# Testing four edge tiles at once for openings in two segment-sum loops on TensorE

## The chip, the cores and the metric

The kernel runs on one core of a Trainium2 chip, as one launch. The metric is the device time of that launch in microseconds. The time of the kernel before is the median of three runs.

## What is computed

A graph layer pair and a routed feed-forward over 3,125 nodes with 768 features and 50,000 edges that are sorted by destination. Two attention layers (eight heads, then one) each gather a row of features for every edge, scale it by the edge's softmax weight and add it up by destination; this sum is what the change touches. The rest is dense. The reference, cut to that:

```python
def gat_layer(x, W, a_src, a_dst, bias, src, dst, heads, out_c, concat):
    h = (x @ W).reshape(n, heads, out_c)
    e = jax.nn.leaky_relu(al_s[src] + al_d[dst], NEG_SLOPE)
    m = jax.ops.segment_max(e, dst, num_segments=n)
    ex = jnp.exp(e - m[dst])
    z = jax.ops.segment_sum(ex, dst, num_segments=n)
    msg = h[src] * (ex / (z[dst] + 1e-16))[:, :, None]
    out = jax.ops.segment_sum(msg, dst, num_segments=n)      # the two aggregations
    return out + bias

x = x + gat_layer(elu(gat_layer(layernorm(x), ..., heads=8)), ..., heads=1)
x = x + routed_ffn(layernorm(x))                             # top 2 of 8 experts
```

## The kernel before

The kernel is a row of parts that follow each other: setup, features, products and scores, `aggregate` (layer one, 8 heads), features and products of layer two, `aggregate_rows` (layer two), the routing and the experts.

Both aggregations work alike. The 50,000 edges are padded to NT = 392 tiles of 128 edges, taken in TURNS = 28 turns of UN = 14 tiles. POOL gathers the 128 rows of a tile by their source numbers into one of 14 buffers (L1473, L1664); it may issue the gather of tile t when TensorE has finished tile t - 13 (the semaphore tile_mm). In `aggregate` VectorE scales the gathered rows by the softmax weights (L1503), which TensorE waits for; in `aggregate_rows` ScalarE puts the weight into the one-hot matrix (L1924, L1931), and TensorE waits for the rows themselves.

TensorE adds a tile up with a one-hot matrix of 64 destinations: `sums` (L1526, L1820) makes two products with f32 operands, one for each half of the row, into one of two banks of accumulators. The 3,200 destinations are 50 groups (windows) of 64. Since edges are sorted, a tile mostly lies in one group. Where a tile reaches into the next group, it opens it: the tile is added once with the old group's one-hots into the old bank (`added`) and once with the next group's into the other bank (`opened`, which also waits for the flush of that bank). In `aggregate_rows` an opening into bank 0 issues besides the router's products (L1845) and the transposes (L1852) of a finished block of 128 destinations.

Which tile opens a group depends on data, so TensorE's sequencer branches. Once per turn it reads a word of 14 bits, `open_bits`, one bit per tile (L1568, L1889). Then the 14 tiles are taken in seven pairs (L1570 and L1891, the loop over k in steps of 2, written out in code). A pair without an opening (L1571: mask and branch) reads the bank register (L1577), branches on it (L1578) and adds both tiles. A pair with an opening reads three numbers of groups from `pair_ends` (L1572, L1893) and runs `single` for both tiles (L1552 to L1565), which has its own branches for the bank and for the groups to open. The same lines stand in `aggregate_rows` some 320 lines further down (L1888 to L1905). The loop over the turns is `pe.Fori` (L1567, L1888): a loop of the sequencer, with one copy of its body in the program.

Of the kernel before, what the change touches and what calls it, by code (L numbers as in the profile page):

```python
# [12 lines left out]
UN = 14  # L13
# [97 lines left out]
def gnn_ffn(nc, io, out):  # L111
    with ExitStack() as ctx:
# [1338 lines left out]
        def aggregate():  # L1451
# [13 lines left out]
            with nc.Block() as block:  # L1465
                @block.gpsimd
                def _(pool):
                    nc.gpsimd.memset(zeros, 0.0).then_inc(zero_set, 1)
                    for t in range(NT):
                        k = t % UN  # L1470
                        if t >= UN:
                            pool.wait_ge(tile_mm, t - UN + 2)
                        pool.indirect_dma_start(rows[k], None, feat_tab[0],  # L1473
                                                bass.IndirectOffsetOnAxis(ap=src_t[:, t:t + 1], axis=0)).then_inc(row_in[k], 16)
# [45 lines left out]
                @block.tensor  # L1520
                def _(pe):
                    def sums(hot, k, bank, start):

                        row = rows[k]
                        for c in range(WPB):
                            m = nc.tensor.matmul(acc[c * WIN:(c + 1) * WIN, bank, 0:HALF], hot, row[:, c * HALF:(c + 1) * HALF],  # L1526
                                                 start=start, stop=True, skip_group_check=True)
                            if c == 0 and not start and k % BATCH == 0:
                                m.then_inc(batch_mm, 1)
                        return m  # L1530

                    def added(i, k, bank):
                        if k % BATCH == 0:
                            pe.wait_ge(hot_ready, i * 2 + (k // BATCH + 1))
                        pe.wait_ge(msg_ready, i * UN + (k + 1))
                        sums(onehot[:, k, :], k, bank, False).then_inc(tile_mm, 1)

                    def opened(b, k, bank):
                        pe.wait_ge(open_ready, b)
                        pe.wait_ge(flushed, b)  # L1540
                        sums(next_x[bank], k, bank, True).then_inc(open_mm, 1)
                    pe.wait_ge(zero_set, 1)
                    for c in range(WPB):
                        m = nc.tensor.matmul(acc[c * WIN:(c + 1) * WIN, 0, 0:HALF], zeros[:, 0:WIN], zeros[:, 0:HALF], start=True, stop=True,
                                             skip_group_check=True)
                    m.then_inc(open_mm, 1)
                    bits_reg = [pe.alloc_register("bits0")]
                    regs = [pe.alloc_register(f"open0_{j}") for j in range(3)]
                    bank_reg = pe.alloc_register("bank0")
                    pe.reg_mov(bank_reg, 0)  # L1550

                    def single(i, k, b0, b1):  # L1552
                        bank = pe.snap(bank_reg, min_val=0, max_val=1)
                        with pe.If(bank > 0):
                            added(i, k, 1)
                        with pe.Else():
                            added(i, k, 0)
                        with pe.If(b1 > b0):
                            with pe.Fori(b0 + 1, b1 + 1) as b:
                                pe.reg_mov(bank_reg, b & 1)  # L1560
                                bank = pe.snap(bank_reg, min_val=0, max_val=1)
                                with pe.If(bank > 0):
                                    opened(b, k, 1)
                                with pe.Else():
                                    opened(b, k, 0)  # L1565

                    with pe.Fori(0, TURNS) as i:  # L1567
                        pe.load(bits_reg, open_bits[0:1, ds(i, 1)])  # L1568
                        bits = pe.snap(bits_reg[0], min_val=0, max_val=(1 << UN) - 1)
                        for k in range(0, UN, 2):  # L1570
                            with pe.If((bits & (3 << k)) > 0):  # L1571
                                pe.load(regs, pair_ends[0:1, ds(i * (UN * 4) + k * 4, 3)])  # L1572
                                b0, b1, b2 = [pe.snap(r, min_val=0, max_val=NW - 1) for r in regs]
                                single(i, k, b0, b1)
                                single(i, k + 1, b1, b2)
                            with pe.Else():
                                bank = pe.snap(bank_reg, min_val=0, max_val=1)  # L1577
                                with pe.If(bank > 0):  # L1578
                                    added(i, k, 1)
                                    added(i, k + 1, 1)  # L1580
                                with pe.Else():
                                    added(i, k, 0)
                                    added(i, k + 1, 0)
                    nc.tensor.matmul(tps[0:32, 0, 0:1], iota_f[:, 0:32], iota_f[:, 0:1], start=True, stop=True,
                                     skip_group_check=True).then_inc(open_mm, 1)

# [31 lines left out]
        def aggregate_rows():  # L1618
# [36 lines left out]
            with nc.Block() as block:  # L1655
# [158 lines left out]
                def _(pe):  # L1814
                    def sums(hot, k, bank, start):

                        row = rows[k]
                        for c in range(WPB):
                            n = CHUNK + ZC if c == WPB - 1 else CHUNK
                            m = nc.tensor.matmul(acc[c * WIN:(c + 1) * WIN, bank, 0:n], hot, row[:, c * CHUNK:c * CHUNK + n],  # L1820
                                                 start=start, stop=True, skip_group_check=True)
                            if c == 0 and not start and k % BATCH == 0:
                                m.then_inc(batch_mm, 1)
                        return m
# [31 lines left out]
                    bank_reg = pe.alloc_register("bank1")  # L1856
                    pe.reg_mov(bank_reg, 0)

                    def added(i, k, bank):
                        if k % BATCH == 0:  # L1860
                            pe.wait_ge(hot_ready, i * 2 + (k // BATCH + 1))
                        pe.wait_ge(row_in[k], i * 16 + 16)
                        sums(onehot[:, k, :], k, bank, False).then_inc(tile_mm, 1)
# [9 lines left out]
                    def single(i, k, b0, b1):  # L1873
                        bank = pe.snap(bank_reg, min_val=0, max_val=1)
                        with pe.If(bank > 0):
                            added(i, k, 1)
                        with pe.Else():
                            added(i, k, 0)
                        with pe.If(b1 > b0):
                            with pe.Fori(b0 + 1, b1 + 1) as b:  # L1880
                                pe.reg_mov(bank_reg, b & 1)
                                bank = pe.snap(bank_reg, min_val=0, max_val=1)
                                with pe.If(bank > 0):
                                    opened(b, k, 1)
                                with pe.Else():
                                    opened(b, k, 0)

                    with pe.Fori(0, TURNS) as i:  # L1888
                        pe.load(bits_reg, open_bits[0:1, ds(i, 1)])  # L1889
                        bits = pe.snap(bits_reg[0], min_val=0, max_val=(1 << UN) - 1)  # L1890
                        for k in range(0, UN, 2):  # L1891
                            with pe.If((bits & (3 << k)) > 0):
                                pe.load(regs, pair_ends[0:1, ds(i * (UN * 4) + k * 4, 3)])  # L1893
                                b0, b1, b2 = [pe.snap(r, min_val=0, max_val=NW - 1) for r in regs]
                                single(i, k, b0, b1)
                                single(i, k + 1, b1, b2)
                            with pe.Else():
                                bank = pe.snap(bank_reg, min_val=0, max_val=1)
                                with pe.If(bank > 0):
                                    added(i, k, 1)  # L1900
                                    added(i, k + 1, 1)
                                with pe.Else():
                                    added(i, k, 0)
                                    added(i, k + 1, 0)
                    pe.wait_ge(xT_ready, NW)  # L1905
                    pe.wait_ge(lg_ready, NW)
                    nc.tensor.matmul(tps[0:32, 1, 400:401], iota_f[:, 0:32], iota_f[:, 0:1], start=True, stop=True,
# [441 lines left out]
```

## Time and profile before

| | |
|---|---|
| time before, median of 3 runs | 2480.03 us (2477.85 to 2483.07) |
| the profiled execution's own time | 2465.81 us |
| its span, first to last instruction | 2464.0 us |
| PE busy, share of the span | 1854.5 us, 75% |
| PEld (weight loads, beside PE) | 985.7 us, 40% |
| DVE busy | 1299.3 us, 53% |
| ACT busy | 712.0 us, 29% |
| POOL busy | 1263.9 us, 51% |
| mean granted TensorE clock | 0.910 |

An engine counts as busy while it executes; register, branch, semaphore and DMA-issuing instructions of the sequencer are not counted. They are in the trace nonetheless, and stand under PEldq for TensorE's sequencer. A matmul's end is modelled. [...]

### The profile page before, as it was taken

The page shows a single profiled execution, that of the slowest core. Times are in us where ns is not written, and L with a number is a line of the kernel's source. Part 1 is how long each engine was busy: PE and PEld are TensorE (multiplying, and loading weights), DVE is VectorE, ACT ScalarE, POOL GpSimd, SP SyncE. Part 2 cuts the span into 40 slices and gives each one's busy share as a digit, 9 for nine tenths or more (in the row PEclk, how much of TensorE's full clock was granted, in tenths as well). Part 3 has the DMA queues.
Part 4 walks back from the last instruction along what each step waited for, and adds up shares of the span by engine and source line. Part 5 has one row for each costly group of instructions (what it writes and reads, how often), then busy time and mean ns, then how long its engine had stood idle before and what let it go on. Part 6 is the DMA issues. An engine that isn't in the chain of part 4 may idle for free. (4 is left out here: it accounts for less than half of the span.)

```text
span 2464.0 us, 32168 instructions
## 1 busy us (share of the span) xinstructions
PE 1854.5 (75%) x8856; PEld 985.7 (40%) x8857; DVE 1299.3 (53%) x2790; ACT 712.0 (29%) x1713; POOL 1263.9 (51%) x1279
## 2 busy tenths in 40 slices
PE   1847887957777777666979867777787784799997
PEld 1325554522222222224635432333333232677775
DVE  7725676836676766667647722343443436422221
ACT  1524433220010001015423333443443441133332
POOL 5065554036666666641051135666666661377775
PEclk9968998978999999897989988999989987899999
DMA  5322321158888888879569978999999986588886
GB/s 177 118 60 57 96 68 43 46 195 288 288 290 289 295 292 284 286 257 290 157 171 289 276 208 274 326 314 312 320 314 320 316 309 227 143 139 135 141 139 103
DMA packets 171459, 533.03 MB, mean 216 GB/s; under 512 B 35106, under 2 KB 66061, under 8 KB 171123
## 3 DMA queue, kind: packets, MB, share of 16 engines
q0 software_dynamic: 99088, 379.24, 53.9%
q1 hardware_dynamic: 61490, 123.21, 14.4%
q10 hardware_dynamic: 10800, 29.70, 3.0%
q8 instruction: 28, 0.46, 0.1%
q14 instruction: 53, 0.43, 0.1%
HBM read 444.94 MB, written 87.10 MB: 216 GB/s over the span
## 5 line engine op out<-in xcount | busy, mean ns | idle before, releaser
L1526 PE MATMUL acc<-ring,work 128*64 128x388 f32 x880 | 206.2, 552 | 83.3 <-issue 55.0
L1820 PE MATMUL acc<-ring,work 128*64 128x384 f32 (+1 forms) x880 | 192.5, 547 | 78.6 <-issue 78.3
L1664 POOL DMA_INDIRECT ring<-feat_tab,src_t x196 | 186.8, 953 | 107.5 <-issue 46.9
L951 PE MATMUL acc<-wg,work 128*128 128x384 f32 x600 | 223.8, 517 | 22.8 <-issue 14.4
L1931 ACT ACTIVATE work<-big,edges 128x64 f32<-128x64 f32 x392 | 135.9, 427 | 345.6 <-DMA edges<-in_w_slow 199.4
L1473 POOL DMA_INDIRECT ring<-feat_tab,src_t x196 | 185.2, 945 | 97.8 <-issue 49.0
L1778 DVE COPY work<-acc 64x384 f32<-64x384 f32 x100 | 56.0, 560 | 310.0 <-DMA ring<-lo_rows 253.5
L2140 POOL DMA_INDIRECT out_rows<-ring,wg x114 | 177.7, 1559 | 79.7 <-ACT ring L2237 56.7
L1503 DVE TENSOR_TENSOR ring<-ring,mps 128x776 f32<-128x776 f32 x196 | 182.9, 959 | 45.7 <-DMA ring<-feat_tab,src_t 33.1
L900 POOL DMA_INDIRECT edges<-score_tab,src_p x152 | 147.9, 973 | 113.2 <-issue 45.4
L1606 ACT ACTIVATE work<-acc 64x388 f32<-64x388 f32 x100 | 48.8, 488 | 514.6 <-DMA edges<-in_a_dst 489.7
L1284 PE MATMUL acc<-wg,work 128*128 128x384 f32 x504 | 184.8, 510 | 9.2 <-issue 7.2
L1526 PE MATMUL acc<-work 128*64 128x388 f32 x504 | 125.0, 548 | 59.9 <-issue 37.5
L1526 PEld LDWEIGHTS acc<-ring,work 128*64 128x64 f32 x880 | 65.4, 147 | 223.5 <-issue 162.4
L951 PEld LDWEIGHTS acc<-wg,work 128*128 128x128 f32 x600 | 114.9, 202 | 90.1 <-issue 34.4
L1820 PE MATMUL acc<-work 128*64 128x384 f32 (+1 forms) x504 | 116.6, 520 | 39.6 <-issue 38.8
L2274 DVE TENSOR_TENSOR edges<-acc,wg 128x192 f32<-128x192 f32 x57 | 20.4, 358 | 238.0 <-PE acc L2174 120.1
L1820 PEld LDWEIGHTS acc<-ring,work 128*64 128x64 f32 x880 | 67.6, 147 | 193.3 <-issue 185.5
L1664 POOL DMA_INDIRECT work<-feat_tab,src_t x112 | 106.5, 951 | 56.5 <-issue 26.9
L1473 POOL DMA_INDIRECT work<-feat_tab,src_t x112 | 105.8, 945 | 56.6 <-issue 26.2
L2174 PE MATMUL acc<-big,work 128*128 x684 | 123.5, 331 | 10.3 <-issue 9.1
L1284 PEld LDWEIGHTS acc<-wg,work 128*128 128x128 f32 x504 | 94.4, 197 | 66.5 <-issue 15.2
(393 smaller groups left out, 3500.7 us busy)
## 6 DMA issues: line engine op xcount, KB each, us to landing
ring<-lo_rows SPq DMA_DIRECT2D x49, 256.0 KB
edges<-in_w_slow SPq DMA_DIRECT2D x28, 384.0 KB, 9.6
edges<-in_w_hebb POOLq DMA_DIRECT2D x28, 384.0 KB, 7.7
edges<-in_w_fast POOLq DMA_DIRECT2D x28, 384.0 KB, 9.1
unit_sum<-edges SPq DMA_DIRECT2D x28, 384.0 KB, 6.7
out_rows<-work SPq DMA_DIRECT2D x52, 192.0 KB
feat_tab<-work ACTq DMA_DIRECT2D x25, 388.0 KB
agg_raw<-work ACTq DMA_DIRECT2D x25, 388.0 KB
```

The source lines that it names most:

```text
L900: pool.indirect_dma_start(src_s[:, t, :], None, score_tab, bass.IndirectOffsetOnAxis(ap=src_p[:, t:t + 1], axis=0)).then_inc(gather_in, 16)
L951: m = nc.tensor.matmul(acc[:, sl * 2 + c, 0:C // 2], xT[sl][:, k, :], wg[:, k, c * (C // 2):(c + 1) * (C // 2)], start=(k == 0), stop=(k = ...
L1284: m = nc.tensor.matmul(acc[:, sl * 2 + c, 0:C // 2], xT[sl][:, k, :], wg[:, k, c * (C // 2):(c + 1) * (C // 2)], start=(k == 0), stop=(k = ...
L1473: pool.indirect_dma_start(rows[k], None, feat_tab[0], bass.IndirectOffsetOnAxis(ap=src_t[:, t:t + 1], axis=0)).then_inc(row_in[k], 16)
L1503: V.tensor_tensor(r3, r3, ex_ps[i % 2][:, k, :].unsqueeze(2).to_broadcast([P, H, HC]), ALU.mult).then_inc(msg_ready, 1)
L1526: m = nc.tensor.matmul(acc[c * WIN:(c + 1) * WIN, bank, 0:HALF], hot, row[:, c * HALF:(c + 1) * HALF], start=start, stop=True, skip_group_ ...
L1664: pool.indirect_dma_start(rows[k][:, 0:C], None, feat_tab[1], bass.IndirectOffsetOnAxis(ap=src_t[:, t:t + 1], axis=0)).then_inc(row_in[k], 16)
L1778: ins = V.tensor_copy(r[w * WIN:(w + 1) * WIN, c * CHUNK:c * CHUNK + n], acc[c * WIN:(c + 1) * WIN, q % 2, 0:n])
L1820: m = nc.tensor.matmul(acc[c * WIN:(c + 1) * WIN, bank, 0:n], hot, row[:, c * CHUNK:c * CHUNK + n], start=start, stop=True, skip_group_che ...
L1931: ins = nc.scalar.activation(onehot[:, j * BATCH + k, :], gaps[j][:, k, :], ACT.Relu, bias=ex[:, first + k:first + k + 1], scale=neg_ex[:, ...
L2140: pool.indirect_dma_start(out[c], bass.IndirectOffsetOnAxis(ap=slots[:, 2, t:t + 1].bitcast(i32), axis=0), y_rows[t % TU][:, c * (C // 2): ...
L2174: m = nc.tensor.matmul(acc[:, 2, 0:HID], xTs[k][:, c, :], big[:, ds(e * HID + c * EH, HID)], start=(c == 0), stop=(c == KC - 1))
```

## The change

The seven pairs of a turn become three fours and a last pair, in both aggregations in the same way. A four is tested as a whole: the mask is 15 instead of 3. Where none of the four tiles opens a group, the bank is tested once and the four tiles are added in a row. Where one of them does, the two pairs are tested and run as before. The old code of the pairs is kept inside each four, and the code for four closed tiles, for either bank, comes beside it. No semaphore, wait or buffer is changed.

```diff
-                        for k in range(0, UN, 2):
+                        def pair(k):
                             with pe.If((bits & (3 << k)) > 0):
                                 pe.load(regs, pair_ends[0:1, ds(i * (UN * 4) + k * 4, 3)])
                                 b0, b1, b2 = [pe.snap(r, min_val=0, max_val=NW - 1) for r in regs]
                                 single(i, k, b0, b1)
                                 single(i, k + 1, b1, b2)
                             with pe.Else():
-                                bank = pe.snap(bank_reg, min_val=0, max_val=1)
-                                with pe.If(bank > 0):
-                                    added(i, k, 1)
-                                    added(i, k + 1, 1)
-                                with pe.Else():
-                                    added(i, k, 0)
-                                    added(i, k + 1, 0)
+                                inside(k, 2)
+
+                        def inside(k, n):
+                            bank = pe.snap(bank_reg, min_val=0, max_val=1)
+                            with pe.If(bank > 0):
+                                for t in range(k, k + n):
+                                    added(i, t, 1)
+                            with pe.Else():
+                                for t in range(k, k + n):
+                                    added(i, t, 0)
+                        for k in range(0, UN - 2, 4):
+                            with pe.If((bits & (15 << k)) > 0):
+                                pair(k)
+                                pair(k + 2)
+                            with pe.Else():
+                                inside(k, 4)
+                        pair(UN - 2)
```

The second hunk, in `aggregate_rows`, is the same text.

## Rows read from the trace of the kernel before

**Rows 1.** Windows: stretch and length us, busy us (count) per engine, PEclk, DMA share, GB/s.
```profile
556.00:1097.00 541.00, 394.09 (x1690) 123.95 (x1686) 376.13 (x451) 55.09 (x140) 349.65 (x370) 0.93 0.86 290
1480.70:1504.10 23.40, 14.98 (x60) 4.95 (x60) 1.34 (x3) 4.21 (x14) 11.22 (x12) 0.79 0.68 217
1504.10:1520.80 16.70, 14.59 (x84) 6.93 (x82) 7.58 (x23) 8.41 (x28) 10.50 (x12) 0.94 0.89 283
1520.80:2051.00 530.20, 408.16 (x2038) 177.66 (x2040) 222.14 (x627) 212.78 (x707) 338.69 (x355) 0.93 0.91 316
```

**Rows 2.** TensorE's sequencer by line: count, duration ns min/median/max, first and last start us.
```profile
L1568 PEldq TENSOR_LOAD <-open_bits x28: 3/307/678, 525.8 to 1081.3; - x28
L1889 PEldq TENSOR_LOAD <-open_bits x28: 5/308/1087, 1479.2 to 2035.1; - x28
L1571 PEldq ALU_OP  x196: 3/36/700, 526.4 to 1097.3; - x196
L1571 PEldq COMPARE_BRANCH  x196: 3/208/1283, 526.5 to 1097.4; - x196
L1577 PEldq MOVE  x147: 3/37/1392, 527.0 to 1095.9; - x147
L1578 PEldq COMPARE_BRANCH  x219: 2/169/2601, 527.1 to 1096.0; - x110
L1572 PEldq TENSOR_LOAD <-pair_ends x49: 13/755/1772, 541.2 to 1097.7; - x49
```

**Rows 3.** Timeline of PE at 1727 us: start us, length us, what.
```profile
1727.62 2.85 PE L1820 MATMUL acc<-ring,work 128*64 128x384 f32 x16 [1.59 <-issue]
```

**Rows 4.** Timeline of POOL, 1710 to 1723 us: start, length, gather, idle before and its releaser.
```profile
1710.34 0.94 POOL L1664 DMA_INDIRECT wg<-feat_tab,src_t  x1 [1.99 <-PE acc L1820]
1711.59 0.95 POOL L1664 DMA_INDIRECT edges<-feat_tab,src_t  x1 [0.31 <-issue]
...
1722.20 0.95 POOL L1664 DMA_INDIRECT ring<-feat_tab,src_t  x1 [2.16 <-DMA ring<-lo_rows]
```

**Rows 5.** Groups by line of PE and PEld: count, busy us, mean ns, idle us before.
```profile
L1526 PE MATMUL acc<-ring,work 128*64 128x388 f32 x880 | 206.2, 552 | 83.3 <-issue 55.0 <-DVE ring L1503 26.9 <-ACT work L1606 0.7
L1526 PE MATMUL acc<-work 128*64 128x388 f32 x504 | 125.0, 548 | 59.9 <-issue 37.5 <-DVE work L1503 17.9 <-DVE wg L1503 2.7
L1526 PE MATMUL acc<-edges,work 128*64 128x388 f32 x256 | 62.4, 525 | 13.4 <-issue 11.7 <-DVE edges L1503 0.8 <-ACT work L1606 0.7
L1526 PE MATMUL acc<-wg,work 128*64 128x388 f32 x124 | 36.5, 558 | 5.1 <-issue 4.5 <-DVE wg L1503 0.4
L1526 PEld LDWEIGHTS acc<-ring,work 128*64 128x64 f32 x880 | 65.4, 147 | 223.5 <-issue 162.4 <-DVE ring L1503 59.0
```

**Rows 6.** Queue q8: whole span; 0-556; 520-556; 1110-1506; 1479-1506; 2055-2464 us.
```profile
q8 instruction: 28, 0.46, 0.1%
q8 instruction: 11, 0.18, 0.2%
q8 instruction: 4, 0.07, 0.8%
q8 instruction: 13, 0.21, 0.2%
q8 instruction: 6, 0.10, 1.4%
q8 instruction: 4, 0.07, 0.1%
```

**Rows 7.** Sequencer branches, short windows at 537, 1480, 1495 and 1498 us: ns min/median/max.
```profile
L1578 PEldq COMPARE_BRANCH  x1: 2601/2601/2601, 537.8 to 537.8; - x1
L1892 PEldq COMPARE_BRANCH  x2: 337/2506/4674, 1479.8 to 1480.8; - x2
L1892 PEldq COMPARE_BRANCH  x1: 2377/2377/2377, 1495.1 to 1495.1; - x1
L1892 PEldq COMPARE_BRANCH  x1: 3502/3502/3502, 1498.2 to 1498.2; - x1
```

More of the change, by code:

```diff
@@ L1890, in _, with pair @@
                         bits = pe.snap(bits_reg[0], min_val=0, max_val=(1 << UN) - 1)
-                        for k in range(0, UN, 2):
+                        def pair(k):
                             with pe.If((bits & (3 << k)) > 0):
@@ L1897, in _, with inside @@
                             with pe.Else():
[L1898 to L1904, printed above, removed]
+                                inside(k, 2)
+                        def inside(k, n):
+                            bank = pe.snap(bank_reg, min_val=0, max_val=1)
+                            with pe.If(bank > 0):
+                                for t in range(k, k + n):
+                                    added(i, t, 1)
+                            with pe.Else():
+                                for t in range(k, k + n):
+                                    added(i, t, 0)
+                        for k in range(0, UN - 2, 4):
+                            with pe.If((bits & (15 << k)) > 0):
+                                pair(k)
+                                pair(k + 2)
+                            with pe.Else():
+                                inside(k, 4)
+                        pair(UN - 2)
                     pe.wait_ge(xT_ready, NW)
```

## The prediction

> **What bounds the kernel now.** I read four views in this order. The windows table gives the two aggregation stages: 541 us of the first one and 530 us of the second go by with POOL, DMA and TensorE all partly busy, none full [rows 1]. The sequencer's rows give the pace: the read of open_bits, one per turn of 14 tiles, runs from 525.8 to 1081.3 us and from 1479.2 to 2035.1 us, 28 times each, so a turn takes 555.5/27 = 20.6 us (the second likewise), 1.47 us per tile [rows 2]. TensorE's own work is far less: where nothing interferes it takes 16 matmuls, four tiles, in 2.85 us, 0.71 us per tile [rows 3]. POOL needs 1.25 us per gather (0.95 busy, 0.30 between), 17.5 us per turn, and makes up the rest of 20.6 us in pauses of about 2 us every eight gathers or so, here one that a TensorE matmul ended [rows 4]. So the pace is a ring: POOL waits for freed rows, TensorE frees them, and TensorE is held up while POOL's gathers run. It isn't TensorE's instruction count: the second stage ran 2,038 matmuls in 530 us, with the router's and the transposes' among them, the first 1,690 in 541 us, at the same pace [rows 1, 2].
> TensorE has a reserve. The second turn of stage two, which starts with rows waiting, took 16.7 us [rows 1]. So it can lose up to 20.6 - 16.7 = 3.9 us per turn before the ring must slow down.
>
> **The change, part by part.** The destinations are sorted, and 49 tiles open a group (the 49 reads of pair_ends [rows 2]), one in eight, so no four tiles hold two openings. Counted from the edge list, 8 of the 49 fall in the last pair of a turn, which keeps its old code; 41 of the 84 fours of each stage have an opening, 43 have none.
> Removed: a four without an opening loses one of two pair tests and one of two bank tests: a mask (36 ns), a branch (208), a move (37), and the bank's branch, at 219 records for 147 pairs, 1.49 times 169 ns [rows 2]. That is 0.53 us, times 43, 23 us per stage.
> Added: a four with an opening pays one more mask and branch and one jump over the other body, at most 36 + 208 + 169 ns = 0.41 us, times 41, 17 us per stage.
> What of it lies on the path: the sequencer runs ahead of the array over closed pairs (four tiles without a pause in [rows 3]), which hides the saving; the 0.41 us stands ahead of the 0.75 us register read [rows 2], where nothing hides it. The ends are all savings and no additions, -46 us for both stages, and the reverse, +34 us. I take -5 us, near nothing, because the pace didn't follow the instruction count above.
>
> The third part is not in the diff's words: **the loop body grows.** A tile's addition is 8 TensorE instructions, four loads and four matmuls (1,764 of each on L1526 for 392 tiles, 49 openings and no more [rows 5]), and one or two for its waits. Each four gets its own body for either bank, 2 x 4 x 9 instructions, with tests and jumps 78, or 80 where a wait for the one-hots falls in: 238 more per loop. The compiled program before has 995 instructions in the first loop and 1,499 in the second.
> What code size costs stands in the instruction queue: q8 brings TensorE's code: four packets in the first turn of stage one, six in that of stage two, 0.10 MB. The windows 0 to 556, 1110 to 1506 and 2055 to 2464 us hold 11 + 13 + 4 = 28, all there are, so none falls in the other 27 turns of either stage [rows 6]. A packet is 16 KB, 256 instructions: 28 packets for the 7,138 instructions, less what was loaded at the start [rows 6]. So code comes in blocks and stays. Where a branch goes to a block that isn't there, the sequencer stands: four branches of the two first turns took 2.60, 4.67, 2.38 and 3.50 us [rows 7], against 0.21 us as a rule [rows 2]. Their places in the program fix the block edges: at every 256th instruction, give or take three, from position 193. Loop two now runs from 4,676 to 6,175: blocks 4545 to 6081, seven of them; the sixth packet is then the block behind the loop, fetched ahead. So the store keeps eight blocks for 27 turns: seven of the loop and one unused.
> After the change loop two starts 238 later and is 238 longer: 4,914 to 6,651. It lies in eight blocks, 4801 to 6593, the last reached by 58 instructions, every turn, since the last pair's code stands there. With the block fetched ahead it wants nine. Loop one (1,950 to 3,183) has six and one ahead and fits.
> No row shows whether a ninth block is kept. If it is, the cost is one more first fetch per stage, 0 to 9 us. If not, the block fetched ahead displaces a block of the loop, most simply the oldest, which is its head, and each of 27 back jumps meets a missing block. The nearest rows price that at 2.38 to 4.67 us; if the head waits behind the block in flight, two in a row, up to 9.3 us [rows 7]. I take 5.6 us, above the middle, because the jump comes within a microsecond or so of entering the last block. Half is swallowed by the reserve of 3.9 us, which can't be all free since the ring also needs POOL's 17.5 us: 2.8 us per turn, times 27, +75 us; with none swallowed 9.3 x 27 = +250, with all 0.
>
> [...]
>
> **Rivals.** (a) *Fits, and the tests were on the path.* The ninth block is kept or not fetched; the saving of 0.53 us per closed four shows in part, 6 to 46 us over both stages. For it: PE's idle time before L1526 is mostly put down to its own issue [rows 5]. Time: about 2480 - 18 = 2462 us. This is the other side of my forecast, and the number of kept blocks decides it. (b) *Fits, and nothing moves:* the change hardly does what it says, because tests run ahead of the array, or the additions eat the saving: 2480 us. (c) *The store is a plain window of eight blocks:* the displaced head displaces the next on its return, and so on round the loop. A turn then meets four or five missing blocks (head, behind each closed four, last pair), 3.3 us on average [rows 7] to 4.67, about 17 us, less 3.9 of reserve: 13 us times 27, +350 us, range +220 to +520: 2830 us. For it: no row of code ever coming back. Against it: nothing either; it takes another rule for replacing. (d) *Forecast: one missing block per turn.*
>
> **Numbers.** Against the profiled execution's own 2465.8 us (its span is 2464.0): -5 (tests) + 3 (first fetches, mostly under the full ring) + 75 (back jumps) = +73 us, 2539. The median of the runs shown is 2480.0, 14 us above the profiled one; I carry that over: 2553 us. Chances: (d) 0.33, with its own range 2490 to 2700; (c) 0.27; (a) 0.25; (b) 0.13; fits but slower, since the additions are exposed, 0.02. The range takes in (d), (b), nearly all of (a) and half of (c): 2452 to 2840. The bound for faster or slower is 0.2%, 5 us, about what a measurement of this kernel can tell from no change: faster 0.25, same 0.13, slower 0.62.
>
> **What would show it.** Packets of q8 in turns 2 to 28 of stage two: about two per turn in (d), six to nine in (c), none in (a) and (b). The longest branches move to the loop's own back jump on the line of the Fori in stage two, at 2.4 to 9 us each, 27 times. Stage one keeps 20.6 us per turn within 0.5 us in all cases but (a), and serves as a control. Records of the pair's mask drop from 196 to 28 + 2 x 41 = 110 per stage, and as many as 84 new ones appear. The prediction fails outright if stage two has no packets after its first turn; its size is wrong if the reserve swallows all (no change at +5 us per turn) or none.

## The result, and the profile after

| | before | after |
|---|---|---|
| median of the runs taken together | 2481.55 us (2477.85 to 2485.82, 4 runs) | 2843.49 us (2842.65 to 2850.68, 4 runs) |
| ratio | | 1.146, 95% interval 1.1438 to 1.1482 |
| span of the profiled execution | 2464.0 us | 2841.6 us |
| mean granted TensorE clock | 0.910 | 0.839 |

The change makes the kernel 15% slower. Nearly all of the loss, 361 of 378 us of the span, falls in the second aggregation. The reads of open_bits, one per turn, of stage one (L1568) and of stage two (now L1899), with count, duration in ns (minimum, median, maximum), first and last start:

```profile
L1568 PEldq TENSOR_LOAD <-open_bits x28: 307/312/1114, 528.2 to 1087.4; - x28
L1899 PEldq TENSOR_LOAD <-open_bits x28: 307/312/849, 1488.7 to 2405.7; - x28
```

Against [rows 2], stage one takes 559.2/27 = 20.7 us per turn (before 20.6), stage two 917.0/27 = 34.0 us (before 20.6). The 27 turns cost 917.0 - 555.9 = 361 us more, 13.4 us each. The rest of the span's 378 us is 9.5 us up to the start of stage two (1488.7 against 1479.2) and 7 us behind its last read.

The code queue of the changed kernel, in the whole span and then in the windows 0 to 560, 1110 to 1485, 1485 to 1512 (the first turn of stage two), 1512 to 2430 and 2430 to 2842 us (packets, MB, share):

```profile
q8 instruction: 272, 4.46, 0.8%
q8 instruction: 12, 0.20, 0.1%
q8 instruction: 7, 0.11, 0.1%
q8 instruction: 6, 0.10, 1.7%
q8 instruction: 243, 3.98, 2.2%
q8 instruction: 4, 0.07, 0.1%
```

Two queues are of the kind "instruction". The other, before and after, in the whole span:

```profile
q14 instruction: 53, 0.43, 0.1%
q14 instruction: 52, 0.43, 0.1%
```

It has 52 or 53 packets in all thirteen runs. q8 has 27 to 30 or 271 to 273, and its count moves with TensorE's code alone: the two kernels of the experiments that differ by 60 of TensorE's instructions, none of them executed, have 28 and 271 packets of q8, and 52 of q14 each. So q8 is read here as the queue of TensorE's code. Each of its packets is 16 KB (4.46 MB / 272).

The whole program before had 28 packets and none in turns 2 to 28 [rows 6]. Now the part of stage two from its first back jump on holds 243, which is 27 x 9. Between 560 and 1110 us, in stage one, there is still none. Where TensorE's sequencer stands meanwhile, by line; L1898 is the loop's own back jump, L1902 the pair's test, L1912 the bank's, L1919 the four's. The last two rows are the pair's and the four's test in stage one, as a measure:

```profile
L1898 PEldq COMPARE_BRANCH  x28: 67/5233/7142, 1512.5 to 2430.2; - x28
L1902 PEldq COMPARE_BRANCH  x110: 67/217/5575, 1499.4 to 2426.1; - x110
L1912 PEldq COMPARE_BRANCH  x157: 65/192/4489, 1493.2 to 2425.5; - x157
L1919 PEldq COMPARE_BRANCH  x84: 68/3911/6345, 1489.3 to 2421.2; - x84
L1571 PEldq COMPARE_BRANCH  x110: 2/208/717, 543.1 to 1103.6; - x110
L1588 PEldq COMPARE_BRANCH  x84: 3/77/705, 528.9 to 1099.6; - x84
```

The 84 tests of a four fall into two kinds: 43 take 3.8 us or more, 41 some 0.08 us, and the median lies between them. 43 is the number of fours without an opening, whose test jumps over the pairs' code; in stage one such a jump takes some 0.2 us. The back jump has a median of 5.2 us. From the first back jump on, the branches over 1.5 us in stage two are 120 with 521.3 us (41 at the fours' test, 40 at a pair's, 27 back jumps, 12 others): 4.4 stalls per turn of 4.3 us each, 19.3 us per turn. Of these 13.4 show in the pace.

The engines, in windows over stage one and stage two (length, busy us and count of PE, PEld, DVE, ACT and POOL, then PEclk, DMA share, GB/s), which answer to [rows 1]:

```profile
560.00:1103.00 543.00, 390.68 (x1686) 127.08 (x1682) 377.16 (x449) 54.58 (x139) 349.67 (x369) 0.93 0.87 288
1485.00:2430.00 945.00, 508.62 (x2196) 248.96 (x2198) 236.80 (x670) 225.58 (x749) 359.33 (x379) 0.71 0.61 193
```

The same view of the kernel before, over the whole of its stage two:

```profile
1485.00:2055.00 570.00, 438.18 (x2193) 190.75 (x2193) 234.54 (x668) 225.41 (x749) 359.47 (x377) 0.93 0.89 309
```

Every engine has idle time. That PE was busy 509 us instead of 438 for as many matmuls is no more work, but a slower clock, as one turn shows. Timeline of PE (start, length, what, idle before it), and under it the windows over four stretches of that turn:

```profile
1781.86 1.71 PE L1830 MATMUL acc<-edges,work 128*64 128x384 f32 x8
1789.89 2.88 PE L1830 MATMUL acc<-ring,work 128*64 128x384 f32 x8 [6.32 <-issue]
...
1803.06 3.68 PE L1830 MATMUL acc<-ring,work 128*64 128x384 f32 x12 [2.90 <-issue]
1806.53 3.80 PE L1830 MATMUL acc<-work 128*64 128x384 f32 x20
1810.14 0.85 PE L1830 MATMUL acc<-wg,work 128*64 128x384 f32 x4
1818.09 2.88 PE L1830 MATMUL acc<-edges,work 128*64 128x384 f32 x8 [7.11 <-issue]
```
```profile
1789.90:1792.70 2.80, 2.80 (x8) 0.72 (x8) 0.00 (x0) 1.17 (x4) 0.95 (x1) 0.50 0.02 9
...
1806.60:1810.20 3.60, 3.52 (x24) 1.78 (x22) 1.34 (x3) 2.73 (x9) 2.69 (x4) 1.00 0.91 311
1818.10:1820.90 2.80, 2.80 (x8) 0.80 (x8) 0.00 (x0) 0.00 (x0) 0.95 (x1) 0.50 0.27 89
```

TensorE stands for 6.32 and for 7.11 us, and this view names "issue" alone for both. TensorE's sequencer stood in branches meanwhile, the back jump in the first gap, a bank's and a pair's test one after the other in the second (duration three times over, in ns, and start):

```profile
L1898 PEldq COMPARE_BRANCH  x1: 5542/5542/5542, 1781.8 to 1781.8; - x1
L1912 PEldq COMPARE_BRANCH  x1: 4489/4489/4489, 1809.5 to 1809.5; - x1
L1902 PEldq COMPARE_BRANCH  x1: 3605/3605/3605, 1814.1 to 1814.1; - x1
```

After each of the two gaps the granted clock is 0.50, and 8 matmuls take 2.88 us (0.36 us each). At 1.00, 20 take 3.80 us (0.19 us each). In [rows 3], 16 took 2.85 us (0.18 us each). So in this turn the matmuls behind a stall also ran at half the pace. POOL's part is seen in the largest group of its gathers in stage two, first before (1485 to 2055 us), then after (1485 to 2430 us). Its idle time, once about evenly "issue" and TensorE, now mostly ends with TensorE:

```profile
L1664 POOL DMA_INDIRECT ring<-feat_tab,src_t x188 | 179.1, 953 | 100.5 <-issue 44.8 <-PE acc L1820 40.6 <-DMA ring<-lo_rows 15.1
L1674 POOL DMA_INDIRECT ring<-feat_tab,src_t x189 | 179.2, 948 | 196.0 <-PE acc L1830 167.8 <-issue 19.8 <-DMA ring<-lo_rows 8.5
```

### The profile page after: what moved, and what is told of

The parts are those of the page before. It is cut to its first block and busy times, and to the rows that moved or that the text cites. A ratio compares the mean times of both kernels' runs of the same rounds, so it can differ in the third digit from the quotient of the medians.

```text
span 2841.6 us, 31925 instructions
## 1 busy us (share of the span) xinstructions
PE 1923.5 (68%) x8856; PEld 1048.3 (37%) x8857; DVE 1303.3 (46%) x2790; ACT 712.8 (25%) x1713; POOL 1262.8 (44%) x1279
## 3 DMA queue, kind: packets, MB, share of 16 engines
q8 instruction: 272, 4.46, 0.8%
## 5 line engine op out<-in xcount | busy, mean ns | idle before, releaser
L1830 PE MATMUL acc<-ring,work 128*64 128x384 f32 x880 | 251.8, 736 | 305.1 <-issue 305.1
L1830 PEld LDWEIGHTS acc<-ring,work 128*64 128x64 f32 x880 | 103.6, 200 | 445.1 <-issue 436.1
L1830 PE MATMUL acc<-work 128*64 128x384 f32 x504 | 124.5, 621 | 67.3 <-issue 67.2
L1674 POOL DMA_INDIRECT edges<-feat_tab,src_t x56 | 53.0, 947 | 233.0 <-PE acc L1830 228.2
L1526 PEld LDWEIGHTS acc<-ring,work 128*64 128x64 f32 x880 | 66.1, 150 | 233.8 <-issue 185.8
L951 PEld LDWEIGHTS acc<-wg,work 128*128 128x128 f32 x600 | 115.3, 202 | 96.4 <-issue 41.2
```

Of the source, the lines that this page charges most:

```text
L951: m = nc.tensor.matmul(acc[:, sl * 2 + c, 0:C // 2], xT[sl][:, k, :], wg[:, k, c * (C // 2):(c + 1) * (C // 2)], start=(k == 0), stop=(k = ...
L1674: pool.indirect_dma_start(rows[k][:, 0:C], None, feat_tab[1], bass.IndirectOffsetOnAxis(ap=src_t[:, t:t + 1], axis=0)).then_inc(row_in[k], 16)
```

## The experiments

The theory under test: the store for TensorE's code keeps eight blocks of 256 instructions. Loop two executes eight blocks after the change and fetches a ninth ahead, behind its end, and with nine wanted in a circle each is dropped before it is wanted again. The rival: the fours themselves cost the time, by their tests, branches or longer bodies, or any growth does. Positions below are counted in the compiled program, and block edges are taken at 193 + 256n, as the prediction read them from the four branches of [rows 7], give or take three; loop two of the changed kernel goes from 4,915 to about 6,635, 42 past the edge at 6,593. "Dead" instructions are matmuls in an `If` that is never entered, so they change the place of code, and add no more than one test per turn. Where that test is inside a loop, the bound of `bits` is widened by one bit for it (not shown). In the code shown, `...` stands for lines or parts of lines left out.

**The same changed code, moved by 168 instructions.** Dead code in front of loop two puts its head at 5,085, behind the edge at 5,057; it then lies in seven blocks, though it is as long as before.

```diff
+                    at_start = pe.snap(bank_reg, min_val=0, max_val=1)
+                    with pe.If(at_start > 0):
+                        for _ in range(42):
+                            nc.tensor.matmul(tps[0:32, 1, 400:401], iota_f[:, 0:32], iota_f[:, 0:1], start=True, stop=True, ...
                     with pe.Fori(0, TURNS) as i:
```

> The changed kernel, with 168 TensorE instructions that are never executed put in front of the second loop, so that its head moves from position 4,915 to 5,085 and its end to about 6,805. The loop is as long as in the changed kernel (some 1,720 instructions), but now lies in seven blocks (5057 to 6593) instead of eight. Theory A (the code store keeps eight blocks, the one fetched ahead counts): stage two falls back to 20.6 us per turn, no code packets after its first turn, 2475 to 2490 us. Rival B (the longer body or the tests and jumps themselves cost the time, wherever they lie): nothing moves, 2840 us. Rival C (the store holds fewer instructions than the body, by length alone): 2840 us too, with nine packets per turn. If A holds, this run is also the price of the tests alone in both stages: 0 to -30 us against the kernel before.

Measured: 2470.10 us against 2467.26 of the kernel before on the same chip, ratio 1.0012 (1.0003 to 1.0021). The whole loss is gone, with every four in place:

```profile
q8 instruction: 30, 0.49, 0.1%
L1904 PEldq TENSOR_LOAD <-open_bits x28: 3/308/1148, 1482.3 to 2040.0; - x28
```

557.7/27 = 20.66 us per turn. The rival falls: what cost 361 us was where the code lay.

**Dead code in the kernel before, 196 and 136 instructions.** Both have the old pairs and one jump over dead code in loop two. With 196 the loop ends at 6,373, past the edge at 6,337, in eight blocks; with 136 it ends at 6,313, in seven.

```diff
                         for k in range(0, UN, 2):
+                            if k == 6:
+                                with pe.If((bits & (1 << UN)) > 0):
+                                    for _ in range(49):                    # 34 in the other
+                                        nc.tensor.matmul(tps[0:32, 1, 400:401], iota_f[:, 0:32], iota_f[:, 0:1], start=True, stop=True, ...
```

> The kernel before with its pairs, and in the body of the second loop 196 TensorE instructions behind a branch that is never taken, with one more mask and branch per turn. The body now ends near 6,373, past the block edge at 6,337, by some 36 instructions: eight blocks and one ahead. A: 27 turns with nine missing blocks each, stage two 33 to 35 us per turn, 2800 to 2860 us, 244 code packets more. B (fours and their tests are the cause): 2480 us, since there are no fours. C (length alone, threshold unknown): either.

> As the run with 196 dead instructions, but 136 of them: the body ends near 6,313, 24 short of the block edge at 6,337, seven blocks. A: no packets after the first turn, 2475 to 2490 us. B: the same. C (length alone, growing with it): between the kernel before and the run with 196, nearer to that one.

Measured: with 196, 2884.28 us, ratio 1.1694 (1.1664 to 1.1724); with 136, 2469.49 us, ratio 1.0015 (1.0005 to 1.0025). The reads of open_bits and the queue, first with 196, then with 136:

```profile
q8 instruction: 271, 4.44, 0.7%
L1889 PEldq TENSOR_LOAD <-open_bits x28: 302/311/643, 1477.4 to 2437.6; - x28
```
```profile
q8 instruction: 28, 0.46, 0.1%
L1889 PEldq TENSOR_LOAD <-open_bits x28: 16/308/1128, 1476.6 to 2035.2; - x28
```

Sixty instructions that are never executed make 415 us: 35.6 us per turn against 20.7. The loss needs no four, and it isn't gradual. Its size is a little above what I expected (33 to 35 us per turn, at most 2860 us).

**The change in one stage alone.** Stage one alone keeps loop two as it was, in seven blocks; stage two alone ends its loop at about 6,397, in eight.

```diff
                         # in the other stage:
-                        for k in range(0, UN - 2, 4): ...
-                        pair(UN - 2)
+                        for k in range(0, UN, 2): ...
```

> The change in the first aggregation alone; the second has the kernel before's pairs again (its head at 4,915, its end near 6,413, seven blocks). Both A and B: no loss in stage two. A: 2475 to 2485 us, stage one 20.6 us per turn as in the kernel before. If the tests are on the path in stage one, 3 to 23 us less than before. B, where a longer body costs by itself: some us more than before.

> The change in the second aggregation alone. Its loop starts where the kernel before's does (4,677) and ends near 6,397, past the edge at 6,337: eight blocks and one ahead. Code store: nine packets per turn, 33 to 35 us per turn, 2820 to 2880 us, the whole loss of the changed kernel. If the loss came from the first stage's longer code or from both together: less than 2700 us.

Measured: stage one alone 2466.78 us, ratio 0.9998 (0.9989 to 1.0007); stage two alone 2824.47 us, ratio 1.1459 (1.1433 to 1.1484), 271 packets, 33.4 us per turn. Where the fours fit they are worth nothing, and where they don't the loss is there in full.

**What the tests are worth.** One kernel puts one more test, an `If` that is never entered, ahead of each pair of the kernel before, 392 in all. Another has the fours in both stages, but takes the pairs' own test out of a four with an opening (it runs four `single`), which makes the code about as long as before.

```diff
                         for k in range(0, UN, 2):
+                            with pe.If((bits & (1 << UN)) > 0):
+                                pe.sem_inc(open_mm, 0) if False else pe.reg_mov(bank_reg, 0)
```
```diff
                             with pe.If((bits & (15 << k)) > 0):
-                                pair(k)
-                                pair(k + 2)
+                                for j in (k, k + 2):
+                                    pe.load(regs, pair_ends[0:1, ds(i * (UN * 4) + j * 4, 3)])
+                                    b0, b1, b2 = [pe.snap(r, min_val=0, max_val=NW - 1) for r in regs]
+                                    single(i, j, b0, b1)
+                                    single(i, j + 1, b1, b2)
```

> The kernel before with one more mask and branch ahead of each pair in both loops (392 of each more, never taken, 0.04 + 0.08 to 0.21 us and the gaps between them), which doubles the pair tests. The second loop still lies in seven blocks. If tests are on the path: 392 x 0.25 to 0.35 = +100 to +140 us, and the change's fours would then be worth 10 to 20 us. If the sequencer runs ahead of the array, or the ring sets the pace: 0 to +10 us, and the fours are worth nothing.

> Fours in both loops, but a four with an opening runs all its four tiles as single ones with their own branches and two reads of the ends, without pair tests. The loops are as short as in the kernel before (the second from 4,659 to about 6,133, seven blocks), so nothing is refetched. Open fours cost some 2 us more of sequencer each (one more read at 0.75 us, two more single tiles at 0.6 us), 41 per stage, closed ones 0.5 us less, 43 per stage. If the sequencer is on the path: +60 to +120 us. If the ring sets the pace: within 10 us of before.

Measured: 392 more tests, 2473.41 us against 2466.77, ratio 1.0027 (1.001 to 1.0044): 6.6 us (2.5 to 10.9), 17 ns each. The added test's rows in stage one:

```profile
L1571 PEldq COMPARE_BRANCH  x196: 3/208/697, 525.6 to 1096.6; - x196
L1571 PEldq ALU_OP  x28: 11/36/712, 525.5 to 1082.6; - x28
```

The mask is taken only once per turn here, so that what each pair gained is the branch alone, which jumps over the body in 208 ns. Over 90% of that is hidden beside the ring. Fours with singles: 2469.31 us, ratio 1.0011 (0.9997 to 1.0025), against the +60 to +120 us that I expected if the sequencer were on the path.

**Does the store hold a window of the program, or any eight blocks?** Here 1,200 dead instructions stand inside loop one (and 36 ahead of it). The loop executes five blocks and, by the theory, fetches two ahead, seven in all, but they lie across ten.

```diff
+                            if k == 6:
+                                with pe.If((bits & (1 << UN)) > 0):
+                                    for _ in range(300):
+                                        nc.tensor.matmul(tps[0:32, 0, 0:1], iota_f[:, 0:32], iota_f[:, 0:1], start=True, stop=True, ...
```

> The kernel before with 36 dead instructions in front of the first loop and 1,200 more behind a never taken branch in the middle of its body (before tile 6), which the sequencer jumps over each turn. The loop lies from 1,988 to 4,184. It touches the blocks 1985 and 2241, jumps over four, and goes on in 3521, 3777 and 4033: five blocks, with those fetched ahead (2497 and 4289) seven; from first to last it spans nine, ten with the one ahead. Theory T (the store holds any eight blocks, by their addresses, and drops the one not used longest): no packets after the first turn, stage one 20.6 us per turn, 2475 to 2490 us. Theory W (a window of consecutive blocks that holds eight): the head is gone at every back jump, nine or ten packets per turn, stage one 30 to 38 us per turn, 2700 to 2950 us. Theory W' (a window, but a jump out of it fetches only what is wanted): four to seven packets per turn.

Measured: 2467.96 us against 2466.77, ratio 1.0011 (0.9998 to 1.0024).

```profile
q8 instruction: 29, 0.48, 0.1%
L1573 PEldq TENSOR_LOAD <-open_bits x28: 3/308/794, 528.0 to 1083.8; - x28
```

Stage one stays at 555.8/27 = 20.6 us per turn, without a packet between 560 and 1110 us. Two pairs of the loop's blocks lie exactly eight apart and don't displace each other. In this run it is the number of blocks that counts, not how far they reach or which place in the store they would share.

**Does a block that is only fetched ahead count?** 136 dead instructions ahead of loop two and 1,160 inside it: seven blocks are executed, and two more are never executed, but lie behind one that is left by a jump, one at the hole and one behind the loop.

> The kernel before with 136 dead instructions in front of the second loop and 1,160 more behind a never taken branch in its body (before tile 6). The loop lies from 4,814 to about 7,475. Each turn executes code of seven blocks only: 4801, 5057, 5313, then over the hole 6593, 6849, 7105, 7361. The blocks behind 5313 and behind 7361 (5569 and 7617) are never executed, only fetched ahead. Theory P (a block fetched ahead takes one of the eight places like any other): 7 + 2 = 9, so nine packets per turn, and stage two at 30 to 36 us per turn, 2720 to 2880 us. Theory U (only executed blocks hold their places, those fetched ahead give way first): none or two packets per turn, 20.6 us per turn, 2475 to 2490 us; under U the changed kernel would fail for its eight executed blocks, and the store would keep seven of them and one ahead.

Measured: 2671.84 us against 2225.28 us of the kernel before on the same chip, ratio 1.2008 (1.1906 to 1.211). The queue in the whole span, then in 1347 to 2270 us, and the two stages' reads:

```profile
q8 instruction: 273, 4.47, 0.7%
q8 instruction: 244, 4.00, 2.0%
L1568 PEldq TENSOR_LOAD <-open_bits x28: 308/314/1180, 455.9 to 934.6; - x28
L1894 PEldq TENSOR_LOAD <-open_bits x28: 307/312/575, 1319.4 to 2243.9; - x28
```

Nine packets per turn again, at 34.2 us per turn against 17.7 in stage one, though only seven blocks are executed. A block fetched ahead took a place like any other here, and was fetched anew each turn. The kernel before is itself 10% faster on this chip (a point for the last section), so the 2720 to 2880 us that I expected don't apply; against that kernel on the same chip the loss is 447 us.

**What sets the pace that hides the tests.** Two kernels leave out part of stage two: one takes half the columns in the matmuls of `added`, the other gathers as many pieces of half a row's length (384 elements, counted by the same numbers in a table of half rows).

```diff
-  m = nc.tensor.matmul(acc[..., bank, 0:n], hot, row[:, c * CHUNK:c * CHUNK + n],
+  m = nc.tensor.matmul(acc[..., bank, 0:n if start else n // 2], hot, row[:, c * CHUNK:c * CHUNK + (n if start else n // 2)], ...
```
```diff
-  pool.indirect_dma_start(rows[k][:, 0:C], None, feat_tab[1],
+  pool.indirect_dma_start(rows[k][:, 0:C // 2], None, feat_tab[1].rearrange("n (a c) -> (n a) c", a=2), ...
```

> Leaves out part of the computation: in stage two the matmuls of `added` take only half of their columns (192 of 384), so half of each sum is missing. Instructions, tests, waits and code length are those of the kernel before. Question: is the matrix work of TensorE in the 20.6 us per turn? If TensorE's array or the reading of its operands set the pace, stage two loses about 0.3 us per tile, 4 us per turn, 110 us in all, and a turn takes 16 to 17 us. If the pace is set by POOL's gathers and the way in which freed rows reach POOL, the turn stays at 20.6 us within 0.5 and the total within 15 us of the kernel before. I expect the second.

> Leaves out part of the computation: in stage two each gather fetches half a row (384 elements of 768), by the same number of gathers, so the other half keeps old values. Question: is the amount of data in the 20.6 us per turn? If the transfer of the rows is on the ring, a turn falls towards POOL's own 14 x 1.25 = 17.5 us, 3 us less, and stage two loses some 85 us; if only the number of gathers and the return of freed rows count, the turn stays at 20.6 us within 0.5. The stage moved 316 GB/s before; I expect a gain of 30 to 85 us.

Measured, on one more chip where the kernel before takes 2225.87 us: half the columns 2228.85 us, ratio 1.0013 (0.9999 to 1.0027); half the rows 2217.81 us, ratio 0.9954 (0.9937 to 0.9971). The reads of open_bits, half columns (stage one, stage two), then half rows (stage two):

```profile
L1568 PEldq TENSOR_LOAD <-open_bits x28: 302/309/1282, 457.1 to 938.4; - x28
L1889 PEldq TENSOR_LOAD <-open_bits x28: 302/317/1109, 1316.4 to 1797.0; - x28
```
```profile
L1889 PEldq TENSOR_LOAD <-open_bits x28: 302/309/1061, 1317.1 to 1788.2; - x28
```

A turn takes 17.8 us in both stages and 17.4 us with half the data: POOL's own 14 x 1.25 = 17.5 us [rows 4]. Half of the data gains 8 us of the 30 to 85 that I expected. Half of the columns gains nothing, but it didn't halve TensorE's time either. The windows 1320 to 1800 us, half columns, then half rows (whose matmuls keep all columns):

```profile
1320.00:1800.00 480.00, 354.26 (x2116) 216.47 (x2118) 228.24 (x644) 223.58 (x744) 354.71 (x372) 0.74 0.97 360
1320.00:1800.00 480.00, 391.90 (x2162) 175.23 (x2160) 230.07 (x649) 225.39 (x749) 359.51 (x378) 0.96 0.70 211
```

TensorE was busy for 354 us instead of 392, at a mean granted clock of 0.74 instead of 0.96. So this run tests 10% less of TensorE's time, not half of it. What speaks for POOL as the pace on this chip is that a turn takes what its 14 gathers take. The 3 us per turn more on the other chips weren't there to be taken apart, so what makes them stays open.

## Why the prediction was wrong

It had the mechanism and chose the wrong one of its two sizes. Point by point:

- **The ring and its pace:** right as a reading (20.6 us per turn), and right that TensorE's instruction count isn't in it: 392 tests more cost 6.6 us. That TensorE's freeing of rows makes the difference between 17.5 and 20.6 us was argued and isn't shown.
- **The tests, -5 us (ends -46 to +34):** stage one alone gave -0.5 us, both stages with the code moved out of the way +2.8 us (by the ratio 0.7 to 5.2), two code packets more included; before that run I had still expected 0 to -30 us. "Near nothing" held. The counts held too: 110 records of the pair's mask and 84 new ones per stage.
- **First fetches, +3 us:** one packet more outside turns 2 to 28 of stage two (29 against 28). Too small to be seen apart.
- **Where the code lies:** I put loop two at 4,914 to 6,651. It lies at 4,915 to about 6,635: the loop grew by 222 instead of 238. Still eight blocks, by 42 instructions instead of 58. This step held, and all hung on it.
- **Whether a ninth block is kept:** no row told, and the 0.60 that (c) and (d) have together was my estimate. For the case that it isn't: "most simply the oldest, which is its head, and each of 27 back jumps meets a missing block". The first half fits the nine packets per turn. The step that failed is the second, the term of **5.6 us per turn with half swallowed, 2.8 x 27 = +75 us**. It stopped after one displacement. But the head, when it comes back, displaces the block that is now the oldest, which is the next one wanted, and so on round the loop: with nine blocks wanted in turn and eight places, dropping the oldest misses all nine. The trace shows exactly nine packets per turn, and the term measured 13.4 us per turn, 13.4 x 27 = 361 us, instead of 2.8 and 75. One miss per turn would need a store that drops some other block than the oldest, and I had named the oldest myself.
- **The rival with that consequence** was rival (c), and its sum came within a few per cent: 17 us of stalls per turn, less 3.9 of reserve, 13 us times 27, 2830 us. Measured were 19.3 us of stalls, 5.9 swallowed, 13.4 us, 2843 us. The four or five stalls were 4.4, at 4.3 us (3.3 to 4.67 forecast). That it came so near is in part luck: the stalls and the part swallowed were both larger than I had them, and the two errors cancel. I called it a "plain window of eight blocks"; the run with the hole in loop one shows that it is no window, but any eight blocks. Its condition should have been read as "the store drops the oldest or least recently used block", which needs no further rule and deserved the larger chance.
- **The reserve of 3.9 us:** I took half of it as usable, and more than all was swallowed, 5.9 us. One turn was also a poor measure of it: in the trace of the kernel before the reads of open_bits in stage two lie 16.3 to 24.1 us apart, and a turn in the middle of the stage took 16.7 us too. The 5.9 us leave out the matmuls that ran at granted clock 0.50 behind the gaps (behind 53 of the 54 over 4 us between 1512 and 2430 us); TensorE was busy 509 - 438 = 71 us longer in stage two, 2.6 us per turn. How the pace divides between stalls and clock these runs don't separate.
- **The control:** stage one stayed within 0.2 us of 20.6 per turn, as said. Its loop has six blocks and one ahead.

The kernels whose loop executes seven and eight blocks, with one ahead, bear out the number eight: 28 q8 packets with 136 dead instructions, 271 with 196. Which block is dropped they don't show: a store that drops the one fetched first and a store that drops the least recently used both miss all nine in a circle.

The end of my range, 2840 us, was 3 us short because it took in only half of a case to which I gave 0.27, and cut it near its centre.

## What to carry to other kernels

Before a loop body of TensorE's sequencer is unrolled, specialised or given a second copy, count its blocks from the compiled positions: those it executes plus each that lies behind a block left by a jump. Up to eight were free here, and the ninth cost 13 to 17 us in every turn in all four kernels that wanted nine. If the loop touches one block more than its length needs, moving it (168 dead instructions ahead of it) can give it all back, and the packets of the instruction queue per turn show at once which side one is on. In all four, one block too many in the circle was paid for with nine packets per turn (271 to 273 in the whole span, against 28), not with one.

## What the runs showed of the hardware that was not expected

- The cost of one block too many is a cliff: 136 unexecuted instructions more, +2.2 us over the whole kernel; 196 more, +417 us.
- Code that is never executed takes a place, if it lies behind a block that is left by a jump (nine packets per turn with seven executed blocks).
- Nine packets bring 16 KB each, so a turn's 147 KB of code is small beside its transfer of rows: 2.2% of the time of 16 DMA engines over 918 us, 1.3 us of one engine per packet. Within the 521 us of stalls a code packet is under way for 214 us. What fills the rest, the profile doesn't say.
- The two gaps of 6.32 and 7.11 us in front of TensorE were each followed by a granted clock of 0.50 for at least the next 2.8 us. The mean over stage two fell from 0.93 to 0.71. With half the columns, at nearly the same pace, it was 0.74, against 0.96 with half the rows.
- The same kernel before took 2467 us on two of the experiments' chips and 2225 us on two others. The turns of an aggregation take 20.6 us on the former and 17.8 us on the latter (read from the run with half the columns, whose total is that of the kernel before). That is some 150 us; another 69 us fall before the first turn of stage one (457.1 us instead of 525.8) and 20 us between the stages, so it isn't a matter of the gathers' ring alone. What differs between these chips, the profile doesn't say.
